# A drain instruction behind each tile's last gather on GpSimd, in the second layer of a two-layer graph network

## The chip, the cores and the metric

The kernel runs on one core of one Trainium2 chip. The metric is the device time of one execution in microseconds, the median of the runs shown. The kernel before takes 1603.69 us (three runs, 1600.84 to 1605.6). A difference is called faster or slower from 0.3% on in the prediction.

## What is computed

The input is `x` (8192 nodes x 128 features, fp32) and `adj` (8192 x 8192, int32, a node pair is an edge with a chance of about 1/1024, so a row has some 8 neighbours). Two layers, each with a residual:

```
h = relu(layernorm(x));  x = x + L0(h, adj)
h = relu(layernorm(x));  x = x + L1(h, adj)

L0:  Kn, Qn = cos_normalize(h Wk^T), cos_normalize(h Wq^T)
     att = softmax over the neighbours of (Kn Qn^T);  result = half (att h) + half h
L1:  g = h W^T + b_W
     e[i,j] = leaky_relu(g[i].a1 + g[j].a2 + b_a, 0.2)
     result = softmax over the neighbours j of e[i,:]  times  g
```

## The kernel before, in words

The adjacency matrix is sparse, so the kernel reads it once, turns each row into a short list of neighbour indices, and gathers the neighbours' rows from a table in HBM. Work goes in T = 64 tiles of P = 128 nodes.

Layer 1 (L0 above) loads and folds the adjacency matrix into lists, projects the features, stores the table `tab0`, gathers from it, and stores the table of the second layer, `tab1`, tile pair by tile pair. A row of `tab1` has ROW = 130 floats: the 128 values of g, the score of the node as a neighbour, and a one, whose weighted sum is the denominator of the softmax.

Each node has K = 5 places of its own for neighbours (`idx_own`). What is beyond five spills into places that the nodes of eight tiles share (`idx_shared`, 27 gathers in eight tiles; `GIVEN` says which of them go with which tile: 4, 4, 3, 3, 4, 3, 3, 3). One gather is one indirect DMA on GpSimd: 128 indices, 128 rows of `tab1`, one row per partition.

Layer 2 is the branch `lists_*` (taken at the end of layer 1 by `either`, unless a list overflowed; then dense code would run). Its order is written out by hand, an in-order program for each engine, with semaphores between them. For tile t:

- GpSimd (`lists_gpsimd`, lines 530 to 545): waits until tile t - 7 has been used (`s_pv1`, the ring `GO` has GR1 = 7 buffers), then issues the tile's 3 or 4 shared gathers into the ring `GS` (line 537) and its 5 own gathers into `GO[t % 7]` (line 542). Each gather raises a semaphore by 16 when its data are there (`s_gs`, `s_go`).
- VectorE (`lists_vector`): `spread_scores` (line 633) waits for the shared gathers and puts their scores on diagonals; for each tile it adds the node's own score and the mask (line 669), takes the own gathers' scores (line 674, which waits for `s_go`), the leaky relu (line 676) and the row maximum (line 678); `finish` (lines 638 to 648) divides the weighted sum of two tiles before and adds the residual.
- ScalarE (`lists_scalar`): copies the transposed weights (line 600), exponentials (line 607), the own weights on diagonals (line 613), and masks ahead (lines 519, 521).
- PE (`lists_tensor`): transposes the shared weights (line 567), multiplies the scores out of the diagonals (line 557), and forms the weighted sum over 5 own and 4 to 6 shared gathers (line 580), which raises `s_pv1`.
- SyncE stores the finished tile (line 526).

Ahead of layer 2, GpSimd waits until all of `tab1` has been stored (line 531). A block of the program (line 935) ends with a drain on every engine and a barrier.

Of the kernel before, what the change touches and what calls it, by code (L numbers as in the profile page):

```python
# [46 lines left out]
def adjacency_layers(nc, x, adj, wq, wk, w, b_w, a_vec, b_a, out):  # L47
# [63 lines left out]
    with ctx:  # L111
# [418 lines left out]
        def lists_gpsimd(pool):  # L530
            second.all_stored(pool)
            for t in range(T):
                (h, u), q = divmod(t, QT), t % GR1
                if t >= GR1:
                    pool.wait_ge(s_pv1, t - GR1 + 1)
                for c in GIVEN[u]:
                    pool.indirect_dma_start(  # L537
                        out=GS[:, (C * h + c) % CR1, :], out_offset=None, in_=tab1,
                        in_offset=bass.IndirectOffsetOnAxis(ap=idx_shared[:, h, c:c + 1], axis=0),
                        bounds_check=None).then_inc(s_gs[u], 16)  # L540
                for s in range(K):
                    pool.indirect_dma_start(  # L542
                        out=GO[q][:, s, :], out_offset=None, in_=tab1,
                        in_offset=bass.IndirectOffsetOnAxis(ap=idx_own[:, t, s:s + 1], axis=0),
                        bounds_check=None).then_inc(s_go[q], 16)

        def lists_tensor(pe):
            pe.wait_ge(s_hm, 1)
# [386 lines left out]
        with nc.Block() as block:  # L935
# [10 lines left out]
            def _(pool):  # L946
# [38 lines left out]
                gather_own(T - 1, 0, 3, s_g[0][(T - 1) % GR])  # L985
                gather_own(T - 1, 3, K, s_last)
                either(pool, lambda e: None, lists_gpsimd)

            @block.tensor
# [672 lines left out]
```

## Time and profile before

| | |
|---|---|
| median of the runs | 1603.69 us |
| the profiled execution: span from the first to the last instruction | 1797.8 us |
| busy in it: PE, PE weight loads, VectorE, ScalarE, GpSimd | 61%, 46%, 59%, 54%, 61% |
| mean granted TensorE clock in it | 0.797 of full speed |
| DMA: moved in the span, mean rate | 358 MB, 199 GB/s |
| queue of GpSimd's gathers (both layers) | 34304 packets, 71.4 MB, 15.2% of 16 engines' span |

The profile is of one execution, and that one was longer than the timed runs: its own time is the span of 1797.8 us, the only time of it that there is. The views name engines as PE, PEld (weight loads), DVE (VectorE), ACT (ScalarE), POOL (GpSimd) and SP (SyncE); a q behind a name is the engine's sequencer. A line number is that of the kernel. Times are in us unless marked ns. A busy share over the whole span mixes stages with different limits. Spans on POOL are rough, and the ends of matmuls are modelled. "issue" is time in which an engine waited for nothing that the profile shows, "remote" a signal whose sender it can't name.

### The profile page before, as it was taken

The numbers are of one execution on the slowest core, as the hardware profiler recorded it, in microseconds if no ns is written. First come the engines' busy times: TensorE is split into PE (matmuls) and PEld (weight loads), VectorE is DVE, ScalarE is ACT, GpSimd is POOL, SyncE is SP. The second block draws the span as 40 slices with busy tenths as digits, with TensorE's granted clock in tenths as the row PEclk, the third lists the DMA queues.
The fourth block names the chain that finished last, engine by engine and source line by source line (L and its number), as shares of the span: only waits on it lengthen the run. The fifth ranks groups of instructions, "written<-read, shape, count | busy, mean of one in ns | idle before, by whom it ended". The sixth has DMA issues, their size and how long they took to land.

```text
span 1797.8 us, 21638 instructions
## 1 busy us (share of the span) xinstructions
PE 1091.8 (61%) x5729; PEld 826.5 (46%) x5729; DVE 1053.4 (59%) x4249; ACT 965.5 (54%) x2795; POOL 1092.0 (61%) x1121
## 2 busy tenths in 40 slices
PE   6883878687867776787756305444444544454546
PEld 4651545455544554555446105444333444344445
DVE  6974678768776777687765114434444444444446
ACT  4653657677766667676667504443433443343334
POOL 1355666666666656566663675766666666666671
PEclk9996879889888887888887556867778767777778
DMA  9998989799979997999921221222222222222221
GB/s 368 421 377 313 345 323 399 289 342 389 393 262 347 358 364 253 344 367 369 360 51 37 52 54 41 55 51 51 52 51 52 54 52 52 51 51 52 53 52 28
DMA packets 90472, 358.43 MB, mean 199 GB/s; under 512 B 23653, under 2 KB 36328, under 8 KB 57576
## 3 DMA queue, kind: packets, MB, share of 16 engines
q1 hardware_dynamic: 49128, 277.05, 39.2%
q0 software_dynamic: 34304, 71.42, 15.2%
q10 hardware_dynamic: 6912, 8.52, 1.3%
q8 instruction: 48, 0.79, 0.2%
q14 instruction: 80, 0.66, 0.1%
HBM read 344.18 MB, written 12.72 MB: 199 GB/s over the span
## 4 chain that ended last, share of the span: by engine, by line
issue 32%; PE 26%; POOL 17%; DVE 7%; ACT 6%; another core or an unknown queue 6%; DMA 5%; SPq 0%; ACTq 0%; POOLq 0%; DVEq 0%
PE ps L580 14%; POOL arena L965 9%; POOL arena L973 6%; DMA arena<-in_adj_dram 3%; PE ps L557 2%; PE ps L1027 2%; PE ps L567 2%; ACT prod L1215 2%; DMA arena<-tab,idx_shared 2%; PE ps L1050 2%; PE ps L1008 1%; ACT diag L1234 1%; POOL arena L542 1%; DVE arena L1443 1%
## 5 line engine op out<-in xcount | busy, mean ns | idle before, releaser
L965 POOL DMA_INDIRECT arena<-tab,idx_own x320 | 329.8, 1030 | 164.5 <-issue 86.5
L580 PE MATMUL ps<-arena,diag 128*128 128x130 f32 x640 | 143.5, 402 | 406.9 <-issue 405.2
L542 POOL DMA_INDIRECT arena<-tab,idx_own x320 | 308.6, 964 | 97.5 <-issue 97.5
L580 PEld LDWEIGHTS ps<-arena,diag 128*128 128x128 f32 x640 | 127.9, 299 | 448.8 <-issue 446.2
L1027 PE MATMUL ps<-arena,fold 128*128 128x512 fp8e4 x1024 | 299.4, 438 | 33.4 <-DMA arena<-in_adj_dram 22.3
L537 POOL DMA_INDIRECT arena<-tab,idx_shared x216 | 206.0, 954 | 181.5 <-remote 101.8
L973 POOL DMA_INDIRECT arena<-tab,idx_shared x216 | 208.9, 967 | 154.3 <-DVE idx_shared L1493 84.3
L600 ACT COPY arena<-ps 128x512 f32<-128x512 f32 (+1 forms) x120 | 52.9, 489 | 459.2 <-remote 395.2
L1050 PE MATMUL ps<-arena,R 128*128 128x154 f32 x736 | 144.8, 357 | 108.5 <-ACT R L1187 38.4
L1215 ACT ACTIVATE prod<-prod,arena 128x128 f32<-128x128 f32 x528 | 203.4, 390 | 0.0
L1050 PEld LDWEIGHTS ps<-arena,R 128*128 128x128 f32 x736 | 133.0, 239 | 133.0 <-issue 50.8
L1027 PEld LDWEIGHTS ps<-arena,fold 128*128 128x128 bf16 x1024 | 102.3, 106 | 188.5 <-issue 84.3
L643 DVE TENSOR_SCALAR share<-ps,none_all 128x1 f32<-128x1 f32 x64 | 13.9, 217 | 266.0 <-remote 239.3
L1197 ACT COPY arena<-ps 128x308 f32<-128x308 f32 (+1 forms) x88 | 40.0, 458 | 232.4 <-remote 114.0
L669 DVE SCALAR_TENSOR_TENSOR arena<-ps,s_all,arena 128x384 f32<-128x384 f32 (+2 forms) x120 | 69.8, 620 | 148.6 <-remote 128.8
L580 PE MATMUL ps<-arena 128*128 128x130 f32 x736 | 138.6, 360 | 0.0
L580 PEld LDWEIGHTS ps<-arena 128*128 128x128 f32 x736 | 136.6, 281 | 0.0
L613 ACT ACTIVATE diag<-ident,arena 128x128 f32<-128x128 f32 x320 | 100.5, 389 | 2.1
L1215 ACT ACTIVATION_READ_ACCUMULATOR prod<-prod,arena 128x1 f32 x528 | 100.6, 190 | 0.0
L1234 ACT ACTIVATE diag<-ident,weight 128x128 f32<-128x128 f32 x315 | 98.0, 386 | 0.1
L1064 PE MATMUL ps<-arena,diag 128*128 128x130 f32 x630 | 85.3, 280 | 6.4 <-issue 6.3
L1062 PEld LDWEIGHTS ps<-arena,Wc 128*128 128x128 f32 x538 | 76.5, 207 | 18.4 <-issue 9.9
(200 smaller groups left out, 2348.3 us busy)
## 6 DMA issues: line engine op xcount, KB each, us to landing
arena<-in_adj_dram SPq DMA_DIRECT2D x256, 1024.0 KB
arena<-tab,idx_own POOLq DMA_INDIRECT x640
arena<-tab,idx_shared POOLq DMA_INDIRECT x432
tab<-arena ACTq DMA_DIRECT2D x16, 260.0 KB, 7.3
tab<-tw ACTq DMA_DIRECT2D x32, 130.0 KB
res<-in_x_dram SPq DMA_DIRECT2D x8, 512.0 KB, 11.7
out_dram<-arena SPq DMA_DIRECT2D x64, 64.0 KB
prod<-in_L_gnn_Wq_dram SPq DMA_DIRECT2D x1, 64.0 KB
```

The costliest lines, as they stand in the source:

```text
L537: pool.indirect_dma_start(out=GS[:, (C * h + c) % CR1, :], out_offset=None, in_=tab1, in_offset=bass.IndirectOffsetOnAxis(ap=idx_shared[:, ...
L542: pool.indirect_dma_start(out=GO[q][:, s, :], out_offset=None, in_=tab1, in_offset=bass.IndirectOffsetOnAxis(ap=idx_own[:, t, s:s + 1], ax ...
L580: last = nc.tensor.matmul(out_ps[p][:, 0:ROW], lhs, rhs, start=s == 0, stop=s == K + n - 1)
L613: last = nc.scalar.activation(diag[p][:, s, :], ident[:, :], ACT.Copy, scale=sc[p][:, s:s + 1])
L965: pool.indirect_dma_start(out=G[t % GR][:, s, :], out_offset=None, in_=tab0, in_offset=bass.IndirectOffsetOnAxis(ap=idx_own[:, t, s:s + 1] ...
L973: pool.indirect_dma_start(out=Gc[:, (C * (t // QT) + c) % CR, :], out_offset=None, in_=tab0, in_offset=bass.IndirectOffsetOnAxis(ap=idx_sh ...
L1027: last = nc.tensor.matmul(keys_ps[t % 2], fold[:, PIECE_BITS * f + b, :], ring8[m % RING][:, b * WORDS:(b + 1) * WORDS], start=False, stop ...
L1050: last = nc.tensor.matmul(E_ps[g % 2][:, k * REC:(k + 1) * REC], R[w % 2][:, at * P:(at + 1) * P], owner[:, w, :], start=w == of[0], stop= ...
L1062: nc.tensor.matmul(pv_ps[p][:, 0:ROW], W[p][j], Gc[:, e, :], start=j == 0, stop=False)
L1064: last = nc.tensor.matmul(pv_ps[p][:, 0:ROW], diag[t % DR][:, s, :], G[q][:, s, :], start=False, stop=s == K - 1)
L1215: last = nc.scalar.activation(prod[p][:, s, :], prod[p][:, s, :], ACT.Copy, scale=norm_of, accum_out=score[p][:, s:s + 1])
L1234: last = nc.scalar.activation(diag[t % DR][:, s, :], ident[:, :], ACT.Copy, scale=weight[t % 4][:, s:s + 1])
```

## The change

In layer 2's program for GpSimd a drain instruction is put behind the last own gather of each tile, inside the loop over the 64 tiles. Nothing else is changed.

```
--- before.py
+++ after.py
@@ -543,6 +543,7 @@
                         out=GO[q][:, s, :], out_offset=None, in_=tab1,
                         in_offset=bass.IndirectOffsetOnAxis(ap=idx_own[:, t, s:s + 1], axis=0),
                         bounds_check=None).then_inc(s_go[q], 16)
+                pool.drain()
 
         def lists_tensor(pe):
             pe.wait_ge(s_hm, 1)
```

## Rows read from the trace of the kernel before

**Rows 1.** Stretches of the span: length, then each engine's busy us (instructions), clock, DMA.
```profile
core 0: us, PE busy (x) PEld busy (x) DVE busy (x) ACT busy (x) POOL busy (x), PEclk, DMA share, GB/s
0.00:122.00 122.00, 97.15 (x494) 68.94 (x494) 101.38 (x476) 71.43 (x169) 38.70 (x49) 0.94 0.98 392
122.00:973.00 851.00, 615.47 (x3273) 426.03 (x3272) 605.98 (x2904) 565.44 (x1940) 538.70 (x536) 0.84 0.84 317
973.00:995.00 22.00, 13.16 (x90) 11.99 (x90) 7.65 (x38) 13.53 (x54) 0.00 (x0) 0.81 0.12 37
995.00:1768.00 773.00, 343.23 (x1710) 299.36 (x1711) 315.67 (x770) 299.16 (x593) 514.60 (x536) 0.72 0.21 52
1768.00:1798.00 30.00, 22.76 (x166) 20.20 (x164) 22.73 (x62) 15.89 (x40) 0.00 (x0) 0.94 0.05 14
```

**Rows 2.** DMA queues from 995 to 1768 us: packets, MB, share of 16 engines.
```profile
q0 software_dynamic: 17152, 35.71, 19.5%
```

**Rows 3.** GpSimd's groups, 995 to 1768 us: count | busy, mean ns | idle before, releasers.
```profile
L542 POOL DMA_INDIRECT arena<-tab,idx_own x320 | 308.6, 964 | 97.5 <-issue 97.5
L537 POOL DMA_INDIRECT arena<-tab,idx_shared x216 | 206.0, 954 | 181.5 <-remote 101.8 <-issue 57.0 <-DMA tab<-tw 22.7
```

**Rows 4.** Timeline, start of layer 2: start, us, instruction [idle before it <-releaser].
```profile
995.23 0.94 POOL L537 DMA_INDIRECT arena<-tab,idx_shared  x1 [22.68 <-DMA tab<-tw]
...
998.98 0.94 POOL L537 DMA_INDIRECT arena<-tab,idx_shared  x1 [0.30 <-issue]
...
1001.52 0.69 DVE L633 TENSOR_TENSOR prod<-ident,arena 128x512 f32<-128x512 f32 x1 [5.12 <-DMA arena<-tab,idx_shared]
...
1010.22 0.94 POOL L537 DMA_INDIRECT arena<-tab,idx_shared  x1 [0.30 <-issue]
...
1012.74 0.69 DVE L633 TENSOR_TENSOR prod<-ident,arena 128x512 f32<-128x512 f32 x1 [10.53 <-DMA arena<-tab,idx_shared]
```

**Rows 5.** Waits from 995 to 1768 us: total us, times, longest.
```profile
PE ps L580 <- issue: 403.2, 57, 42.6
ACT arena L600 <- remote: 395.2, 53, 12.2
...
POOL arena L537 <- remote: 101.8, 28, 10.8
```

**Rows 6.** Timeline, GpSimd's last tile.
```profile
1756.46 0.94 POOL L537 DMA_INDIRECT arena<-tab,idx_shared  x1 [2.92 <-remote]
...
1765.22 0.94 POOL L542 DMA_INDIRECT arena<-tab,idx_own  x1 [0.30 <-issue]
```

**Rows 7.** Chain that ended last, the tail: start, us, what.
```profile
1773.44 1.15 DVE arena L669 x2
...
1778.90 1.15 DVE arena L669 x2
...
1795.27 0.35 DVE arena L648
```

**Rows 8.** Line 935, the block's end: count, duration ns min/median/max, first and last start.
```profile
L935 POOLq DRAIN  x1: 16524/16524/16524, 1756.2 to 1756.2; - x1
...
L935 DVEq DRAIN  x1: 391/391/391, 1795.3 to 1795.3; - x1
L935 SPq DRAIN  x1: 7/7/7, 1797.6 to 1797.6; - x1
```

**Rows 9.** The program's first instructions on GpSimd, same columns.
```profile
L1650 POOLq DRAIN  x1: 187/187/187, 0.3 to 0.3; - x1
L1650 POOL MEMSET const-uint8-127<- x1: 118/118/118, 0.3 to 0.3; 128x1 uint8 x1
```

**Rows 10.** Timeline of GpSimd around a wait for the ring.
```profile
1317.06 0.94 POOL L542 DMA_INDIRECT arena<-tab,idx_own  x1 [0.30 <-issue]
1321.12 0.94 POOL L537 DMA_INDIRECT arena<-tab,idx_shared  x1 [3.11 <-remote]
1322.37 1.00 POOL L537 DMA_INDIRECT arena<-tab,idx_shared  x1 [0.30 <-issue]
```

More of the change, by code:

```diff
@@ L545, in lists_gpsimd @@
                         bounds_check=None).then_inc(s_go[q], 16)
+                pool.drain()
         def lists_tensor(pe):
```

## The prediction, made before the change was run

> **What bounds the kernel now.** I read the profile from the outside in: first the busy times by stage, then GpSimd's groups and waits in layer 2, then the order of single instructions at the start and at the end of layer 2, last the sequencer's drains.
>
> The stage table [rows 1] splits the profiled execution: prologue to 122 us, gathers of layer 1 to 973 us, a joint of 22 us, layer 2's gathers from 995 to 1768 us, a tail of 30 us. The change touches the fourth stage alone. There no engine is full: PE is busy 343 us of 773, GpSimd (POOL) 515, and the DMA engines have a share of 0.21. The gather queue itself takes 19.5% of the engines' time [rows 2], so bytes bound nothing.
>
> GpSimd's groups [rows 3] are 320 + 216 = 536 gathers, 8.375 for each of the 64 tiles, with 308.6 + 206.0 = 514.6 us busy, 0.96 us each. Between two gathers 0.30 us pass with nothing to wait for. At the start of the stage [rows 4] one gather follows the other every 1.25 us; 536 of them make 669.5 us. The other idle time is 101.8 us in 28 waits [rows 5] for the weighted sum of seven tiles before, which frees the ring: 2.92 us of idle time ahead of the last tile's first gather [rows 6]. The same view puts 403 us of PE's idle time to no cause and 395 us of ScalarE's to a signal it can't name; in the profiled execution signals between the engines come late.
>
> Can that hold in the timed runs? Their median is 1603.7 us, 194.1 less than the span of 1797.8. Layer 2's first gather starts at 995.2 [rows 4]; with 669.5 us of gathers and nothing else, and the tail of 30 us [rows 1], 1694.7 us result, 91 over the median. So the timed runs have no room for GpSimd's 101.8 us of waits, and some of the cadence or of layer 1 must be shorter there too. If layer 1 is as long as profiled, layer 2 has 1603.7 - 995.2 - 30 = 578.5 us, 9.0 us a tile, 1.08 us a gather: between the gather's own 0.96 and the profiled 1.25. What could take 9.0 us a tile? The chain through VectorE, ScalarE and PE, once no gather is left, runs a tile in 1778.90 - 1773.44 = 5.46 us [rows 7]. GpSimd's 8.375 gathers at no less than 0.94 take 7.9. I conclude that GpSimd's queue is what layer 2 waits for in the timed runs, and that a pause on it goes to the end undiminished.
>
> **The change part by part.** Nothing is removed or moved. Sixty-four drains are added, one behind each tile's last gather. Queued behind each on GpSimd's sequencer are the next tile's wait and its 8 or 9 gathers; everyone in layer 2 waits for these. Without a drain the sequencer hands gathers over ahead of their execution: the drain that closes the program began at 1756.2, when the last tile's first gather had not started (1756.46) [rows 6, 8]. With one, the next tile's gathers can be handed over only when it has ended.
>
> So the pause per tile is (end of the last gather's row to end of the drain) + (release to start of the next gather) - (0.30 that lie there today). For the second term: release at 1756.2, start at 1756.46 [rows 6, 8], some 0.2 us. For the first the trace has no drain between gathers, only bounds:
> - Low: the drain ends with the engine's last instruction. VectorE's closing drain ended at 1795.3 + 0.39 = 1795.7, its last instruction at 1795.27 + 0.35 = 1795.6 [rows 8, 7]; GpSimd's drain behind four memsets took 0.19 us, about as long as one of them [rows 9]. That makes 0.05 + 0.2 - 0.3, nothing: between -0.1 and +0.1 us a tile. A gain beyond that I exclude, because the same gathers run in the same order with nothing between them removed.
> - High: GpSimd's closing drain lasted 16.52 us and ended at 1772.7 [rows 8], 6.6 us behind the end of the last gather at 1765.22 + 0.94 = 1766.16 [rows 6]. That makes 6.6 + 0.2 - 0.3 = 6.5 us a tile.
> - Between: the drain waits until the gather's data have landed. VectorE, which waits for the fourth gather of tile 0, starts at 1001.52, 1.6 us behind that gather's end at 999.92; for tile 1 it starts at 1012.74 behind 1011.16, again 1.6 us [rows 4]. That makes 1.6 + 0.2 - 0.3 = 1.5 us a tile.
>
> The only drain behind gathers, the closing one, did not end with the engine's last row, so I leave the low end. It is the row nearest in kind, but not in place: it stands behind 1072 gathers with no drain among them, whereas each new one stands behind the 8 or 9 since the one before. If the closing drain goes through what has piled up, little of its 6.6 us comes back every tile, and the landing is left. I take 1.5 us, and 1.1 to 2.2 as its own range.
>
> The sum: 63 pauses lie between tiles; the 64th, behind the last gather, lies beside the tail and costs nothing. 63 x 1.5 = 94.5 us. In the profiled execution GpSimd's stage would be 669.5 + 94.5 = 764 us against the 771 that it takes from 995.2 to 1766.2, because there the 101.8 us of ring waits give way first; of its own 1797.8 us, a profile after could therefore make 1791 (all waits gone) to 1892 (none gone). In the timed runs there are no such waits to give way: 1603.7 + 94.5 = 1698 us, with 1673 to 1742 from 1.1 and 2.2 us.
>
> By the Trainium skill, PSUM — Partial Sum Buffer, section Engine vs sequencer instructions, a drain waits for the engine to go fully idle. By the Trainium skill, Perfetto Trace Analysis, section DMA Instruction — SWDGE (GPSIMD), a gather's row ends when the last descriptor is written, not when the data are there. Taken together they give the low bound, and no loss; the trace disagrees at its only such drain, which outlasted the last gather's row by 6.6 us.
>
> **The rivals.**
> 1. The drain is nothing: it ends with the last gather's row, or does no more than SyncE's 7 ns [rows 8]. For: VectorE's and the first GpSimd drain [rows 7 to 9]. Against: the closing one. Time: 63 x (-0.1 to +0.1), 1598 to 1610 us.
> 2. The drain costs what the closing one did, each time: 63 x 6.5 = 410, 2014 us. For: the one row there is. Against: that it stands behind 1072 gathers.
> 3. Not slower: the timed runs are paced like the profiled one, by PE's weighted sums through the ring, and GpSimd waits there too. A wait of about 3.1 us comes with every second tile, one of them in [rows 10], and two drains of 1.5 us fit into it: about 1604 us, and if the pause lets late signals through, up to the 101.8 us less. It decides from the point where the other engines need more than 8.375 gathers + 1.5 us a tile, 10.5 us at a cadence of 1.08. For: the profile's waits. Against: the 91 us above, and the 5.46 us a tile at the end.
>
> **How the numbers follow.** Forecast 0.58, rival 1 0.12, rival 2 0.18, rival 3 0.12. A difference under 0.3%, 4.8 us, can't be told from none. Faster comes from a quarter of rival 3, 0.03. Same: rival 1 and the rest of rival 3 less their edges, 0.18. Slower: the forecast, rival 2 and those edges, 0.79. The range takes in the forecast's own 1673 to 1742, rivals 1 and 3 at its low side, and drains up to 3 us (63 x 3 = 189 us) at its high side: 1600 to 1790. Out are most of rival 2 and the gains.
>
> **What would show it.** The profile after has a drain line with 64 instructions that end 1.6 to 1.8 us behind the last gather's end of their tile, and a gap of 1.8 us instead of 0.30 ahead of every tile's first gather. GpSimd's waits for the ring shrink. Gaps near 0.3 us speak for rival 1, near 6.8 for rival 2. The prediction is wrong if the gaps are there and the time is not (rival 3: the bound in the timed runs was misread), or if the price of one drain lies outside 1.1 to 2.2 us.

## The result, and the profile after

The changed kernel takes 1757.32 us (four runs, 1756.8 to 1759.61), the kernel before, run beside it, 1602.79 us (four runs): 154.5 us more. The ratio on record is 1.0974 with a 95% interval of 1.0961 to 1.0987 (the two medians alone give 1.0964). Forecast were 94.5 us more. The time lies in the stated range, 1600 to 1790, but above the forecast's own 1673 to 1742.

The profiled execution of the changed kernel spans 1755.0 us, close to its timed runs. That of the kernel before, on which the prediction rests, was not: 1797.8 us. So the kernel before was profiled once more in the experiments, spanning 1601.1 us, and where after is held against before below, that second profile is meant.

The stretches of the span, of the changed kernel first and then of the kernel before, second profile; the columns are those of [rows 1]:

```profile
122.00:868.00 746.00, 575.02 (x3273) 405.48 (x3273) 598.55 (x2901) 565.91 (x1942) 535.62 (x536) 0.90 0.94 361
868.00:890.00 22.00, 14.61 (x90) 13.27 (x90) 8.64 (x41) 13.11 (x52) 0.62 (x2) 0.73 0.13 39
890.00:1742.00 852.00, 387.78 (x1820) 323.44 (x1821) 332.26 (x807) 309.81 (x618) 530.76 (x536) 0.71 0.21 47
1742.00:1755.00 13.00, 6.86 (x57) 6.17 (x55) 7.70 (x25) 5.29 (x15) 0.00 (x0) 0.96 0.07 20
```

```profile
122.00:868.00 746.00, 575.37 (x3274) 404.44 (x3272) 599.18 (x2901) 565.49 (x1941) 531.72 (x535) 0.90 0.94 361
868.00:890.00 22.00, 14.69 (x90) 13.36 (x90) 8.65 (x41) 13.53 (x55) 0.94 (x1) 0.73 0.14 40
890.00:1588.00 698.00, 375.64 (x1813) 313.77 (x1814) 333.23 (x807) 309.42 (x618) 532.85 (x536) 0.75 0.27 57
1588.00:1601.00 13.00, 7.46 (x63) 6.85 (x61) 7.79 (x25) 5.47 (x15) 0.00 (x0) 1.00 0.07 20
```

Layer 1 and the joint take as long in both (layer 2's first gather starts at 890.0 and at 890.5 us), and so does the tail behind the last gather (14.7 us). The stretch of layer 2's gathers grows from 698 to 852 us, by 154. Its 536 gathers are busy for the same 531 to 533 us. What grew is the time between them. GpSimd's groups for layer 2, after and then before (second profile), columns as in [rows 3]:

```profile
L542 POOL DMA_INDIRECT arena<-tab,idx_own x320 | 326.9, 1022 | 97.5 <-issue 97.5
...
L537 POOL DMA_INDIRECT arena<-tab,idx_shared x216 | 203.9, 944 | 243.5 <-issue 170.9 <-PE ps L581 51.2 <-DMA tab<-tw 21.4
```

```profile
L542 POOL DMA_INDIRECT arena<-tab,idx_own x320 | 329.0, 1028 | 97.5 <-issue 97.5
...
L537 POOL DMA_INDIRECT arena<-tab,idx_shared x216 | 203.9, 944 | 86.9 <-issue 64.3 <-DMA tab<-tw 21.4 <-PE ps L580 1.2
```

The idle time ahead of the shared gathers, where a tile begins, goes from 86.9 to 243.5 us: 156.6 us more, against 154.5 in the time. The 51.2 us that the view puts to PE's line 581 are 19 of the same pauses, 2.7 us each, in which a PE signal happened to come last: in all 63 pauses the next gather starts 0.71 us behind the drain's end, so the ring added nothing. In the kernel before the same place shows 64.3 us with no cause, 0.30 each, and the 1.2 us put to PE are four more gaps of 0.30: GpSimd does not wait for the ring in layer 2. The 101.8 us of [rows 3, 5] belonged to that one execution.

One pause, GpSimd's last two tiles in the changed kernel (columns as in [rows 4]), then the drains of the loop and of the block's end (columns as in [rows 8]):

```profile
1726.55 0.95 POOL L542 DMA_INDIRECT arena<-tab,idx_own  x1 [0.30 <-issue]
1730.11 0.94 POOL L537 DMA_INDIRECT arena<-tab,idx_shared  x1 [2.61 <-issue]
...
1738.84 1.51 POOL L542 DMA_INDIRECT arena<-tab,idx_own  x1 [0.30 <-issue]
```

```profile
L546 POOLq DRAIN  x64: 8670/9227/18742, 889.7 to 1733.1; - x64
...
L936 POOLq DRAIN  x1: 53/53/53, 1742.4 to 1742.4; - x1
```

The median pause (the idle time ahead of a tile's first gather) is 2.69 us where 0.30 lay before. A drain's row is not its price: the row begins when the sequencer reaches the drain, with gathers still to run (the first at 889.7, before layer 2's first gather at 890.0), so what counts is how far its end lies behind the last gather's. The last drain of the loop ends where the block's drain starts, at 1742.4, 2.0 us behind the last gather's end at 1740.35; the block's drain then takes 0.05 us, where in [rows 8] it lasted 16.5, 6.6 of them behind the last gather. One drain of the loop is twice as long as the others, 18.7 us: the first one, of which more below.

What a drain waits for can be read tile by tile. The trace records 16 semaphore signals for each gather; the last of them is taken as its landing. In the 62 tiles behind the first that have a pause, the tile's last gather landed 1.52 to 2.71 us behind the end of its row, and the drain ended 0.36 to 0.41 us behind that landing each time (correlation 0.99). The tile that landed latest has the longest of these pauses:

```profile
1632.17 1.22 POOL L542 DMA_INDIRECT arena<-tab,idx_own  x1 [0.30 <-issue]
1637.18 0.94 POOL L537 DMA_INDIRECT arena<-tab,idx_shared  x1 [3.78 <-issue]
```

Its 3.78 us are 2.71 to the landing, 0.36 to the drain's end and 0.71 to the next gather.

### The profile page after: what moved, and what is told of

The parts are those of the page before. It is cut to its first block, busy times and chain, and to the rows that moved or that the text cites. A ratio compares the mean times of both kernels' runs of the same rounds, so it can differ in the third digit from the quotient of the medians.

```text
span 1755.0 us, 21702 instructions
## 1 busy us (share of the span) xinstructions
PE 1080.7 (62%) x5729; PEld 817.5 (47%) x5729; DVE 1048.6 (60%) x4249; ACT 965.8 (55%) x2795; POOL 1105.7 (63%) x1121
## 4 chain that ended last, share of the span: by engine, by line
DMA 28%; PE 26%; POOL 19%; issue 14%; DVE 8%; ACT 3%; POOLq 1%; SPq 0%; ACTq 0%; DVEq 0%
DMA arena<-in_adj_dram 17%; PE ps L581 12%; DMA arena<-tab,idx_shared 10%; POOL arena L537 8%; PE ps L558 5%; POOL arena L966 5%; PE ps L1028 4%; POOL arena L974 3%; POOL arena L542 2%; DVE prod L634 2%; PE ps L1051 1%; ACT prod L1216 1%; PE ps L1063 1%; POOLq L546 1%; PE ps L1065 1%
## 5 line engine op out<-in xcount | busy, mean ns | idle before, releaser
L558 PE MATMUL ps<-prod,column 128*128 128x384 f32 (+1 forms) x128 | 113.9, 994 | 462.5 <-DVE prod L634 462.5
L537 POOL DMA_INDIRECT arena<-tab,idx_shared x216 | 203.9, 944 | 243.5 <-issue 170.9
L608 ACT ACTIVATE arena<-arena,negm 128x773 f32<-128x773 f32 (+1 forms) x64 | 58.5, 914 | 533.8 <-DVE negm L680 533.8
L1028 PE MATMUL ps<-arena,fold 128*128 128x512 fp8e4 x1024 | 284.1, 413 | 101.7 <-DMA arena<-in_adj_dram 101.2
L634 DVE TENSOR_TENSOR prod<-ident,arena 128x384 f32<-128x384 f32 (+3 forms) x70 | 39.7, 574 | 501.4 <-DMA arena<-tab,idx_shared 501.4
L558 PEld LDWEIGHTS ps<-prod,column 128*128 128x128 f32 x128 | 32.1, 311 | 477.6 <-issue 436.5
L581 PEld LDWEIGHTS ps<-arena,diag 128*128 128x128 f32 x640 | 148.5, 326 | 50.3 <-issue 47.0
L1051 PE MATMUL ps<-arena,R 128*128 128x154 f32 x736 | 126.8, 328 | 52.6 <-ACT R L1188 52.6
L581 PE MATMUL ps<-arena,diag 128*128 128x130 f32 x640 | 145.1, 409 | 3.0 <-ACT diag L614 3.0
L581 PE MATMUL ps<-arena 128*128 128x130 f32 x736 | 117.4, 320 | 0.0
L581 PEld LDWEIGHTS ps<-arena 128*128 128x128 f32 x736 | 116.7, 244 | 0.0
```

The lines of the kernel that those rows point to most:

```text
L537: pool.indirect_dma_start(out=GS[:, (C * h + c) % CR1, :], out_offset=None, in_=tab1, in_offset=bass.IndirectOffsetOnAxis(ap=idx_shared[:, ...
L558: last = nc.tensor.matmul(T_ps[t % 4][:, 0:n * P], column[:, 0:1].to_broadcast([P, P]), on_diag[t % 2][:, 0:n, :], start=True, stop=True)
L581: last = nc.tensor.matmul(out_ps[p][:, 0:ROW], lhs, rhs, start=s == 0, stop=s == K + n - 1)
L1028: last = nc.tensor.matmul(keys_ps[t % 2], fold[:, PIECE_BITS * f + b, :], ring8[m % RING][:, b * WORDS:(b + 1) * WORDS], start=False, stop ...
L1051: last = nc.tensor.matmul(E_ps[g % 2][:, k * REC:(k + 1) * REC], R[w % 2][:, at * P:(at + 1) * P], owner[:, w, :], start=w == of[0], stop= ...
```

## The experiments

Eight kernels ran. Unless said otherwise an edit stands in the kernel before, behind the gather of line 542 in the loop over the tiles, where the changed kernel has its drain. "Behind" is counted from the end of the last gather's row.

**The kernel before, profiled again** (no edit).

> The kernel before, profiled once more, because its first profiled execution (span 1797.8 us) was 194 us longer than its timed runs. Theory: a profiled execution without late signals spans within 1% of the median of 1602.8 us; layer 2's first gather starts near 890 us (it did at 890.0 in the profile of the changed kernel), the gathers follow at 1.25 us, 536 of them make 669.5 us, and GpSimd's waits for the ring are below 40 us in total. Rival: the waits of about 100 us are there again, and the timed runs are paced by the ring.

Measured: one time of 1603.17 us, span 1601.1. The first gather of layer 2 starts at 890.5 us, none of the gaps between gathers is over 0.6 us, and VectorE, ScalarE and PE hang on the gathers:

```profile
ACT arena L607 <- DVE negm L679: 379.1, 64, 8.2
DVE prod L633 <- DMA arena<-tab,idx_shared: 346.0, 64, 10.4
PE ps L557 <- DVE prod L633: 316.7, 64, 9.0
```

Each row (who waits <- for whom: total us, times, longest) has 64 waits, one for each tile, and they form a chain: ScalarE for VectorE, PE for VectorE, VectorE for a gather that lands. So GpSimd's queue is the bound with no slack, and the rival of a pace set by the ring falls. The gathers take 695.9 us from the first start to the last end, 1.30 us each. Against the first profile, the first gather of layer 2 starts 105 us sooner, the gathers take 75 us less and the tail 17: layer 1, the waits and the tail were shorter, not the gathers' cadence.

**A semaphore wait instead of the drain.**

```
+                pool.wait_ge(s_go[q], go_before[q] + 16 * K * (t // GR1 + 1))
```

> In place of the drain, GpSimd waits on the semaphore of the tile's own gathers, which tells that their data have landed. Theory (the drain costs more than the landing): the gap ahead of a tile's first gather is 1.6 (landing seen by a waiting engine) + 0.2 (restart of a gather that is already parked behind its wait) = 1.8 us instead of 2.69, so 63 x (1.8 - 0.3) = 95 us over before, 1697 us. Rival 1 (a wait for the landing costs the same as a drain, whatever its means): gap 2.7, 1753 us. Rival 2 (the handing over ahead is lost in either case): gap 1.6 + 0.7 = 2.3, 1729 us.

Measured: 1705.58 us, 101.5 over before (ratio 1.0629, 1.0612 to 1.0647).

```profile
1199.79 0.94 POOL L542 DMA_INDIRECT arena<-tab,idx_own  x1 [0.30 <-issue]
1202.57 0.94 POOL L537 DMA_INDIRECT arena<-tab,idx_shared  x1 [1.84 <-DMA arena<-tab,idx_own]
```

The pause is 1.84 us here, 1.9 in the mean: the next gather starts 0.26 us (median) behind the landing's last signal. So waiting for the landing costs about what the prediction said a drain would (94.5 us); the drain costs 0.8 us more a tile, and with its dear first one 53 us more in all. Both rivals (1753 and 1729 us) fall.

**Drains set apart**, behind six tiles.

```
+                if t in (0, 1, 3, 7, 15, 31):
+                    pool.drain()
```

> Drains behind tiles 0, 1, 3, 7, 15 and 31 alone, so that 545, 9, 16, 33, 67 and 134 gathers lie between a drain and the one before (or the program's start). In the changed kernel the first drain ended 7.59 us behind the last gather's end, all later ones 1.98. Theory (a drain goes through what was issued since the last one): the six end about 7.6, 2.0, 2.0 to 2.1, 2.2 to 2.4, 2.5 to 4 and 3 to 7.6 us behind, rising with the count; and the closing drain, 270 gathers later, 4 to 7.6 us. Time: 8 + 2.4 x 2 + 3 x 3 = about 22 us over before, 1625 us. Rival (the first drain of layer 2 is special, for instance code that is loaded once): 7.6 and five times 2.0, the closing one 2.0; 8 + 5 x 2.4 = 20 us, 1623 us. The time can't tell these, the drains' ends can.

Measured: 1634.9 us, 30.8 over before (1.0183, 1.0164 to 1.0202). GpSimd's first gather behind each of the six drains:

```profile
911.51 0.95 POOL L537 DMA_INDIRECT arena<-tab,idx_shared  x1 [8.31 <-issue]
...
925.14 0.94 POOL L537 DMA_INDIRECT arena<-tab,idx_shared  x1 [2.69 <-issue]
...
948.92 0.95 POOL L537 DMA_INDIRECT arena<-tab,idx_shared  x1 [2.96 <-issue]
...
995.02 0.95 POOL L537 DMA_INDIRECT arena<-tab,idx_shared  x1 [3.75 <-issue]
...
1088.46 0.94 POOL L537 DMA_INDIRECT arena<-tab,idx_shared  x1 [6.23 <-issue]
...
1270.61 0.94 POOL L537 DMA_INDIRECT arena<-tab,idx_shared  x1 [7.29 <-issue]
```

With 545, 9, 16, 33, 67 and 134 gathers since the drain before, the pauses are 8.31, 2.69, 2.96, 3.75, 6.23 and 7.29 us: from 9 to 134 they rise with what was issued since the last drain. The place in the layer does not do it: in the changed kernel the pauses have a median of 2.68 us in the first half of the layer and 2.69 in the second. The rival (2.69 five times) falls. The time was a miss, 30.8 us over before where 22 were expected: the two longest pauses behind the first came to 6.2 and 7.3 us and had been put at some 3.

Past a hundred gathers there is no steady rise. Behind the last gather, or behind its own start where that came later, a drain ended 9.3 us after 268 gathers (this run's closing one), 5.9 after 527 (the closing one of the run with a drain behind the first tile), 6.9 after 536 (the drain ahead of layer 2, next run), 7.6 after 545 (behind the first tile, where no drain came before), 8.3 after 554 (the first one of the run with a drain behind every second tile), and 6.6 after 1072 (the closing ones of the kernel before, of the nop and of the semaphore wait). Where the same count came more than once (545 and 1072) the figures agree to 0.01 us, so it is no scatter; why it rises and falls stays open.

**One more drain, ahead of layer 2**, in the changed kernel.

```
+                pool.drain()
                 either(pool, lambda e: None, lists_gpsimd)
```

> The changed kernel with one more drain on GpSimd, ahead of the branch at the end of layer 1, where GpSimd sits idle for some 20 us anyway. Theory (the first drain pays for all gathers of layer 1): the added drain takes the 7.6 us in the shadow, the first drain of layer 2 ends 2.0 us behind its last gather, and the time is 5.6 us below the changed kernel's 1757.3: 1751.7 us. Rival (what is dear is the first drain of layer 2): it keeps its 7.6 us, time 1757 us.

Measured: 1758.32 us, 154.2 over before (1.0947, 1.0931 to 1.0963).

```profile
902.90 0.95 POOL L542 DMA_INDIRECT arena<-tab,idx_own  x1 [0.30 <-issue]
906.65 0.95 POOL L537 DMA_INDIRECT arena<-tab,idx_shared  x1 [2.80 <-issue]
```

The first pause of layer 2 shrinks from 8.3 to 2.80 us, as the theory has it; the added drain ended 6.9 us behind, in the shadow of the joint. Whether the time falls by the expected 5.6 us is not settled: by the medians it does not (154.2 us over before here, 154.5 in the changed kernel), by the ratios (1.0947 against 1.0974) it falls by some 4 us, with intervals that touch. The other pauses of this profile are 2.4 us longer in sum. Layer 2's first gather started at 892.9 us in it, 2.9 later than in the changed kernel's, but 892.3 to 892.8 also come without that drain. Whether it holds the start back stays open.

**Memsets between the last gather and the drain.**

```
+                nc.gpsimd.memset(keys[:, :, :], 0.0)
+                nc.gpsimd.memset(fold[:, :, :], 0.0)
+                pool.drain()
```

> The changed kernel with two memsets of idle buffers on GpSimd between a tile's last gather and the drain, so that the engine is busy while the gather's data land (1.28 us behind the gather's end). Theory (a drain waits for the engine and for the landing of every gather before it, then goes through the gathers issued since the last drain, some 0.3 to 0.7 us): if the memsets last over 1.3 us, the drain ends at most 0.8 us behind their end. Rival (a drain behind gathers takes a fixed 2.0 us from when the engine has nothing left): it ends 2.0 us behind their end. The time is 63 x (length of the memsets + drain's rest + 0.7 - 0.3) over before and is no test by itself.

Measured: 1823.6 us, 222.3 over before (1.1393, 1.1376 to 1.1409).

```profile
1019.62 0.95 POOL L542 DMA_INDIRECT arena<-tab,idx_own  x1 [0.30 <-issue]
1020.56 0.54 POOL L546 MEMSET keys<- 128x512 f32 x1
1021.02 1.82 POOL L547 MEMSET fold<- 128x2048 bf16 x1
1024.35 0.95 POOL L537 DMA_INDIRECT arena<-tab,idx_shared  x1 [1.50 <-issue]
```

The memsets follow the gather without a pause and end 2.28 us behind it, later than the landing (1.6 us behind it in the median). From their end to the next gather 1.50 us pass here, 1.42 in the median; 0.71 of that is the restart, the time from the drain's end to the next gather, so the drain ended 0.71 us (median) behind the memsets, not 2.0. The rival of a fixed price falls: behind 9 gathers a drain waits for a landing that runs beside the engine's own work, and 0.7 us of its own are left. What layer 1 left behind does not run beside it. The first drain of this run:

```profile
900.29 1.83 POOL L547 MEMSET fold<- 128x2048 bf16 x1
910.42 0.95 POOL L537 DMA_INDIRECT arena<-tab,idx_shared  x1 [8.31 <-issue]
```

Its pause is the same 8.31 us as without memsets, counted from their end.

**A nop instead of the drain.**

```
+                pool.nop()
```

> A sequencer instruction that waits for nothing (a nop) in place of each drain. Theory (only the wait and the end of handing gathers over ahead cost): no gap over 0.6 us between gathers, time within 0.3% of before, 1604 us. Rival (any instruction of the sequencer between two tiles breaks the hand-over): gaps of 0.7 us ahead of each tile, 63 x 0.4 = 25 us, 1629 us.

Measured: 1601.84 us, ratio 1.0000 (0.9991 to 1.0009).

```profile
L537 POOL DMA_INDIRECT arena<-tab,idx_shared x216 | 203.8, 944 | 88.1 <-issue 65.2 <-DMA tab<-tw 22.6 <-PE ps L581 0.3
```

No pause: idle ahead of a tile's first gather is what it was. One more instruction on the sequencer that does not wait costs nothing here.

**A drain behind every second tile.**

```
+                if t % 2:
+                    pool.drain()
```

> A drain behind every second tile (32 of them). From the drains set apart: behind 16 or 17 gathers a drain ended 1.0 us behind the landing, behind 9 it was 0.7. Theory (landing 1.28 + 0.31 + 0.043 us for each gather since the last drain, restart 0.71): gap 3.0 us, 31 x 2.7 = 84, and 5 us once for what layer 1 left: 89 us over before, 1693 us. Rival 1 (a fixed price per drain): 31 x 2.39 + 6 = 80 us, 1684 us. Rival 2 (the price goes with the gathers alone): 150 us, 1754 us.

Measured: 1692.62 us, 91.3 over before (1.0572, 1.0557 to 1.0587).

```profile
1039.56 0.94 POOL L542 DMA_INDIRECT arena<-tab,idx_own  x1 [0.30 <-issue]
1043.57 0.94 POOL L537 DMA_INDIRECT arena<-tab,idx_shared  x1 [3.07 <-issue]
```

Pauses of 3.04 us in the median, as worked out from the drains set apart. Half the drains cost 59% of the price: a part for each drain, and a part for each gather since the last one.

**One drain, behind the first tile.**

```
+                if t == 0:
+                    pool.drain()
```

> One drain, behind the first tile of layer 2. Theory: its gap is 8.3 us in place of 0.3 (the drain goes through what layer 1 issued), nothing follows, and GpSimd's queue is what the layer waits for without slack: 8.0 us over before, 1612 us. Rival 1 (the one-time part is hidden, since the other engines have yet to begin): 2.4 us, 1606.5 us, not to be told from no change. Rival 2 (the ring's lead of seven tiles makes it good): no difference.

Measured: 1610.16 us, 8.9 over before (1.0054, 1.0042 to 1.0066).

```profile
L547 POOLq DRAIN  x1: 18731/18731/18731, 892.6 to 892.6; - x1
```

```profile
902.77 0.94 POOL L542 DMA_INDIRECT arena<-tab,idx_own  x1 [0.31 <-issue]
912.02 0.94 POOL L537 DMA_INDIRECT arena<-tab,idx_shared  x1 [8.31 <-issue]
```

The drain ends at 892.6 + 18.7 = 911.3 us, 7.6 behind the gather's end at 903.7, and 0.7 before the next start at 912.02. One pause of 8.31 us at the very start of the layer, 8.0 more than before, appears in the time (by the interval 6.7 to 10.6 us): neither the ring's lead of seven tiles nor the other engines' late start hides it.

In all of them the time follows GpSimd's pauses. Idle ahead of line 537 less the joint's wait, over the 65.5 us of before, against the time over before:

| kernel | pauses, us | time, us |
|---|---|---|
| changed kernel | +156.6 | +154.5 |
| semaphore wait | +102.3 | +101.5 |
| every second tile | +91.0 | +91.3 |
| drain ahead of layer 2 as well | +153.5 | +154.2 |
| six drains apart | +29.4 | +30.8 |
| first tile alone | +8.0 | +8.9 |
| nop | 0.0 | +0.6 |

The intervals of the times reach some 2 to 3 us to either side. With memsets ahead of the drain, pauses of 78.8 us more and 63 x 2.28 us of memsets make 222.4, against 222.3 measured.

## Why the prediction was right, and where its size was off

The prediction named two signs of being wrong. The first, pauses that are there and a time that is not, did not come. The second did: a drain behind a tile costs 2.69 - 0.30 = 2.39 us, outside the 1.1 to 2.2 us that it gave. The time lies in the stated range only because that range also took in drains of up to 3 us.

- **The bound.** Right in the conclusion: GpSimd's queue, with no waits to give way in the timed runs, and every pause goes to the end (the table). The working was half wrong. It let layer 1 be as long as profiled and shortened the cadence to 1.08 us a gather; the second profile has 1.30 us a gather and a layer 1 that ends 105 us sooner. With that start and a tail of 14.7 us, 1603.7 leaves 698 us for gathers that make 669.5 at the cadence used: some 29 us of room, so the argument that the median leaves none for waits does not hold by itself. That rows of up to 1.5 us fill this room, and not waits, only the second profile shows. The other leg holds: 5.46 us a tile for the other engines, against 10.9 for GpSimd's gathers.
- **The pauses.** 63, undiminished, the 64th beside the tail: right. Rival 1 (a drain that is nothing) and rival 3 (the ring's waits swallow it) are excluded by the pauses and by the time.
- **The landing, 1.6 us.** Right as the time to the landing (1.59 us, the median over the tiles), and right for a wait on it: 94.5 us forecast, 101.5 measured with the semaphore. (The 1.28 us that two of the expectations put for the landing are the 1.98 less a 0.7 of the drain's own; the signals do not bear them out.) But the landing was taken as all that a drain does. The drains of the loop end 1.98 us behind (median), 0.36 us behind the landing. This term was mis-sized: 0.4 us a tile, 24 us in all.
- **The restart, 0.2 us.** This is the term that was mis-sized most. 0.2 was read from a gather parked behind a semaphore wait [rows 6, 8]. It holds behind such a wait (0.26 us in the run with the semaphore). Behind a drain it is 0.71 us, in every run with one: 0.5 us a tile, 32 us in all. That the next gather can't be handed over before the drain has ended, which the prediction said, is likely the cause; it was not tried by itself.
- **What has piled up.** Seen as the reason why the closing drain's 6.6 us would not come back every tile, and right: rival 2 (2014 us) falls, and the drains set apart show the pile. But the sum gave it no price. The first drain of layer 2 pays for all of layer 1, 5.6 us once, and no longer does with a drain ahead of the layer. Why what has piled up takes the time that it takes is not shown.

So 63 x (1.98 + 0.71 - 0.30) = 150.6, and 5.6 once, make 156 us, against 154.5 measured. The forecast was 60 us short: the drain's own rest makes 24 of it, the restart 32, the pile 6, which is 2 more than was missing.

The Trainium skill, PSUM — Partial Sum Buffer, section Engine vs sequencer instructions, says that a drain waits until the engine is fully idle. The runs here agree only if the data of the gathers it has issued count as part of the engine: the loop's drains ended 0.36 to 0.41 us after the data had landed, and 2.0 us (median) after the engine's last row.

## What to carry to other kernels

Where a queue is the bound, price an instruction put on it by what it makes the queue wait for and by how long the next one takes to start behind it, and look for the first instance apart from the rest: it may pay for all that went before. If the queue must know that gathers have landed, a wait on their own semaphore cost 1.6 us a tile here and a drain 2.4. And hold a profile's span against the timed runs before its waits are believed: the 101.8 us of waits in the first profile were not there in the second.

## What was not expected of the hardware

GpSimd's drain behind gathers is no fixed cost. With 9 gathers issued since the last drain it ended 0.36 us behind their landing, 2.0 us behind the last gather, or 0.71 us behind memsets that outlast the landing. With 16, 33, 67 and 134 it ended 2.25, 3.0, 5.5 and 6.6 us behind the last gather (each is the pause less the restart of 0.71), and past that it goes up and down with the count, from 5.9 to 9.3 us, the same to 0.01 us where the count was the same. The 7.6 us for 545 gathers begin when the engine's last instruction ends: they stood behind the memsets as well. The block's own drain, behind a drain, took 0.05 us.
